# Delta layer: beta sigmoids moved, v times beta moved, chunk sums read from PSUM banks, unread matmuls around the norms

## What is computed

```python
q = _causal_dwconv(x @ Wq, conv_q)      # four taps, then silu; k and v alike
q = q / norm(q);  k = k / norm(k)       # over the 32 of a head
beta = sigmoid(x @ Wb)                  # one per head
Kb, Vb = K * beta, V * beta
A = einsum('bnihd,bnjhd->bnij', Kb, K)
T = inverse-like triangular matrix, row by row from I - tril(A, -1)
W = T @ Kb;  U = T @ Vb
# over the chunks of 64, Sd = diagonal of S:
u_i = u0 - w_i * Sd;  o = q_i * Sd + tril(sum(q_i * k_i)) * u_i
S = S + einsum('bchd,bche->bhde', k_i, u_i)
out = (o * rsqrt(mean(o * o) + EPS) * g) @ Wo
```

## Time and profile before

| what | value |
|---|---|
| time, median of 3 runs | 1680.47 us (1678.34 to 1684.89) |
| the profiled execution | 1683.24 us |
| its span on the core | 1681.5 us |
| mean granted TensorE clock over the span | 0.914 |
| delta layer in it | 1264 to 1464 us |

### The profile page before, as it was taken

How to read it: one execution, slowest core, us unless ns; L and a number is a source line. 1 busy time by engine, 2 the same in 40 slices (tenths; PEclk the granted TensorE clock), 3 DMA queues, 4 the chain that set the end, 5 groups by cost and what they waited for, 6 DMA issues and landing times. The chain is left out here.

```text
span 1681.5 us, 26802 instructions
## 1 busy us (share of the span) xinstructions
PE 1382.7 (82%) x9088; PEld 941.8 (56%) x9088; DVE 1180.0 (70%) x2866; ACT 774.6 (46%) x1412; POOL 731.4 (43%) x921
## 2 busy tenths in 40 slices
PE   4699999956996539997799898899994588389998
PEld 3333333244884327873477676677872377276886
DVE  5877777456556674558799898697778644769776
ACT  2277777730222221216887664545554311064654
POOL 3833332025642017620088787066672141006665
PEclk9699999968997869998899999999997699589999
DMA  1244240000100000100011110564530000164543
GB/s 39 65 116 130 77 139 24 2 26 13 38 26 12 0 26 26 38 13 19 22 45 41 35 45 20 214 134 123 134 105 7 0 1 1 25 216 120 139 131 106
DMA packets 77883, 104.76 MB, mean 62 GB/s; under 512 B 25185, under 2 KB 43121, under 8 KB 77233
## 3 DMA queue, kind: packets, MB, share of 16 engines
q1 hardware_dynamic: 77760, 103.23, 21.7%
HBM read 92.81 MB, written 10.39 MB: 61 GB/s over the span
## 5 line engine op out<-in xcount | busy, mean ns | idle before, releaser
L526 DVE CUSTOM_DVE_ANT_1 la_neg<-bank,la_table 128x512 f32<-128x512 f32 x256 | 166.4, 688 | 41.5 <-PE bank L617 40.8
L1699 POOL TENSOR_TENSOR lh_h_low<-lh_hidden,lh_h_high 128x512 fp32r<-128x512 f32 x84 | 111.3, 1327 | 161.9 <-ACT lh_h_high L1732 161.6
L1412 DVE TENSOR_TENSOR_SCAN le_h<-le_keep,bank 128x512 f32<-128x512 f32 x128 | 152.2, 1209 | 24.0 <-issue 19.6
L1497 PEld LDWEIGHTS bank<-le_diag,le_dtxT 128*128 128x128 f32 x1024 | 125.6, 191 | 57.8 <-issue 41.7
L1699 POOL TENSOR_TENSOR lf_h_low<-lf_hidden,lf_h_high 128x512 fp32r<-128x512 f32 x84 | 111.1, 1325 | 106.6 <-ACT lf_h_high L1732 106.3
L1497 PE MATMUL bank<-le_diag,le_dtxT 128*128 128x128 f32 x1024 | 132.4, 277 | 21.2 <-DVE le_h L1412 13.6
L453 ACT ACTIVATE la_probT<-bank 128x512 f32<-128x512 f32 x256 | 135.6, 605 | 11.4 <-PE bank L636 9.3
L1722 ACT ACTIVATE bank<-bank 128x512 f32<-128x512 f32 x144 | 83.7, 582 | 62.0 <-PE bank L1887 60.3
L1345 ACT ACTIVATE le_keep<-le_dt,le_A 128x512 f32<-128x512 f32 x128 | 87.1, 711 | 17.5 <-DVE le_h L1412 17.5
L1255 POOL TENSOR_TENSOR le_hc<-le_h,le_c_row 128x512 f32<-128x512 f32 x64 | 81.4, 1272 | 30.0 <-issue 20.5
L48 PE MATMUL bank<-ident 128*128 128x512 bf16 x142 | 45.2, 489 | 59.0 <-DVEq L830 40.4
(11 more groups left out here) (570 smaller groups left out, 3611.7 us busy)
## 6 DMA issues: line engine op xcount, KB each, us to landing
lf_weight<-lf_scratch SPq DMA_DIRECT2D x128, 128.0 KB, 3.0
lh_weight<-lh_scratch SPq DMA_DIRECT2D x128, 128.0 KB, 3.2
le_c_row<-le_scratch SPq DMA_DIRECT2D x32, 256.0 KB, 3.1
la_table<-la_scratch SPq DMA_DIRECT2D x4, 1792.0 KB, 7.0
lf_weight<-lf_scratch SPq DMA_DIRECT2D x64, 64.0 KB, 2.2
lh_weight<-lh_scratch SPq DMA_DIRECT2D x64, 64.0 KB, 2.2
la_bias_parts<-la_scratch_parts SPq DMA_DIRECT2D x12, 248.0 KB, 6.2
lb_w1s<-in_L_ffn_w_dram SPq DMA_DIRECT2D x8, 256.0 KB, 2.8
```

Of the source, the lines that this page charges most:

```text
L526: dve.tensor_tensor_reduce(out=neg[:, u % 2, :].rearrange("p (c i) -> p c i", i=P), in0=k.bank[u % RING1][:].rearrange("p (c i) -> p c i", ...
L1412: dve.tensor_tensor_scan(h[:, i, :], keep[:, i, :], k.bank[4 + q % 2][:], 0.0, ALU.mult, ALU.add).then_inc(scanned, 1)
L1497: last = pe.matmul(k.bank[4 + q % 2][:, j * P:(j + 1) * P], dtxT[:, (g * G2 + bb) * TPB + j, c, :], diag[:, d % DIAGS, j, :], start=True, ...
L1699: pool.tensor_tensor(h_low[:, u % RING, :], hidden[:, u % RING, :], h_high[:, u % RING, :].bitcast(F32), ALU.subtract)\
```

## The change

The sigmoids of beta, with their matmuls, go behind the projections of batch 0, and v times beta ahead of the reciprocals. PE gets 14 idle products behind the last convolution, before the norm sums, and 12 more behind the first root, before the spread. W and U go to eight different banks. Of each, only the four first columns of every chunk are copied (`w_first`, `u_first`, 128x32); the product with k reads the bank itself, and batch by batch W and U alternate.

```diff
-        prod = sb("prod", [P, T])
+        prod = sb("prod", [P, 2, T])
+        w_first = sb("w_first", [P, B, NCH, B])
+        u_first = sb("u_first", [P, B, NCH, B])
...
                     act.activation(xp[:, i, b, TAPS - 1:], k.bank[4 + n % 4][:], ACT.Copy).then_inc(in_copied, 1)
-                if b:
+                if b == 0:
+                    for c in range(B):
+                        act.wait_ge(beta_done, c + 1)
+                        act.activation(beta[:, c, :], k.bank[c][:], ACT.Sigmoid).then_inc(beta_ready, 1)
+                else:
                     silu_and_squares(b - 1)
             silu_and_squares(B - 1)
-            for b in range(B):
-                act.wait_ge(beta_done, b + 1)
-                act.activation(beta[:, b, :], k.bank[b][:], ACT.Sigmoid).then_inc(beta_ready, 1)
...
             for b in range(B):
-                act.wait_ge(wu_done, b + 1)
-                act.activation(wT[:, b, :], k.bank[b % 2][:], ACT.Copy).then_inc(w_copied, 1)
-            for b in range(B):
...
+            for b in range(B):
+                dve.wait_ge(act_ready, 3 * (b + 1))
+                dve.wait_ge(beta_ready, b + 1)
+                dve.tensor_tensor(s3[:, 2, b, :], s3[:, 2, b, :], beta[:, b, :], ALU.mult).then_inc(vb_ready, 1)
             dve.wait_ge(act_ready, 3 * B)
...
-            for b in range(B):
-                dve.tensor_tensor(s3[:, 2, b, :], s3[:, 2, b, :], beta[:, b, :], ALU.mult).then_inc(vb_ready, 1)
...
-                dve.tensor_copy(uT[:, b, :], k.bank[2 + b % 2][:]).then_inc(u_copied, 1)
-            dve.wait_ge(u_copied, B)
-            dve.wait_ge(w_copied, B)
-
-            for src, dst in ((wT, ka), (uT, kbv)):
-                for b in range(B):
-                    link(dve.tensor_tensor(prod[:], s3[:, 1, b, :], src[:, b, :], ALU.mult))
-                    link(dve.tensor_reduce(dst[:, b, :], prod[:].rearrange("p (n c) -> p n c", c=CH), AX_X, ALU.add))
+                for i, (bank, dst, start) in enumerate(((k.bank[b], ka, w_first), (k.bank[4 + b], kbv, u_first))):
+                    dve.tensor_copy(start[:, b, :, :], bank[:].rearrange("p (n c) -> p n c", c=CH)[:, :, 0:B])
+                    link(dve.tensor_tensor(prod[:, i, :], s3[:, 1, b, :], bank[:], ALU.mult))
+                    last = dve.tensor_reduce(dst[:, b, :], prod[:, i, :].rearrange("p (n c) -> p n c", c=CH), AX_X, ALU.add)
+                link(last)
...
+                if b == 0:
+                    pe.wait_ge(wbr_ready, 1)
+                    pe.wait_ge(norm.xnT_ready, B)
+                    for c in range(B):
+                        pe.matmul(k.bank[c][:], wbr[:].rearrange("p h d -> p (h d)"), k.xnT[:, c * T:(c + 1) * T], start=True, stop=True)\
+                          .then_inc(beta_done, 1)
...
+            pe.wait_ge(conv_ready, 3 * B)
+            k.idle_products(pe, 14, 3)
             pe.wait_ge(sq_ready, 2 * B)
             lengths(k.bank[0], sq, norm_done)
             lengths(k.bank[1], sq_k, norm_done)
+            pe.wait_ge(root_ready, 1)
+            k.idle_products(pe, 12, 3)
...
-                if b >= 2:
-                    pe.wait_ge(w_copied, b - 1)
-                    pe.wait_ge(u_copied, b - 1)
-                for src, bank in ((kbn, k.bank[b % 2]), (vbn, k.bank[2 + b % 2])):
+                for src, bank in ((kbn, k.bank[b]), (vbn, k.bank[4 + b])):
```

More of the change, by code:

```diff
@@ L2026, in layer_delta @@
         sq_k = wT
-        uT = beta
         o = cT
@@ L2039, in layer_delta @@
                                                                           sem("yT_done"), sem("m_ready"), sem("mT_ready"))
-        t_ready, wu_done, w_copied, u_copied = sem("t_ready"), sem("wu_done"), sem("w_copied"), sem("u_copied")
+        t_ready, wu_done = sem("t_ready"), sem("wu_done")
         qk_ready, qk_done, o_ready, osq_ready, on_done, oroot_ready, on_ready, out_done = (
@@ L2221, in _ @@
                 sdb = bcast(sd[:, b, 0:1], (1, NCH), (0, B))
-                last = dve.tensor_tensor(u0[:, b, :, :], first(wT[:])[:, b], sdb, ALU.mult)
+                last = dve.tensor_tensor(u0[:, b, :, :], w_first[:, b, :, :], sdb, ALU.mult)
             link(last)
-            link(dve.tensor_tensor(u0[:], first(uT[:]), u0[:], ALU.subtract))
+            link(dve.tensor_tensor(u0[:], u_first[:], u0[:], ALU.subtract))
             link(dve.tensor_tensor(u0[:], u0[:], early[:], ALU.mult))
@@ L2253, in _ @@
                     pe.matmul(k.bank[4 + n % 4][:], w3[:, i, :], k.xnT[:, b * T:(b + 1) * T], start=True, stop=True).then_inc(in_done, 1)
-            pe.wait_ge(wbr_ready, 1)
-            for b in range(B):
-                pe.matmul(k.bank[b][:], wbr[:].rearrange("p h d -> p (h d)"), k.xnT[:, b * T:(b + 1) * T], start=True, stop=True).then_inc(beta_done, 1)
+                if b == 0:
[4 more added lines that the diff above has]
+                          .then_inc(beta_done, 1)
             pe.wait_ge(pool_order, 2 + 3 + 1 + B)
```

## The result

The changed kernel took 1676.95 us at the median of 20 runs (1671.82 to 1686.72), the kernel before 1684.91 us at the median of 20 (1673.87 to 1688.06). The ratio on record, which is not the quotient of these two medians, is 0.9962, with a 95% interval of 0.9949 to 0.9976: 0.38% faster, 6.4 us, and no change is outside the interval. The two medians themselves lie 7.96 us apart, and that too is inside the interval (4.0 to 8.6 us). A second set of seven runs, beside the last experiments, gave 0.9933 (0.9907 to 0.9959); its expectation was

The account below looks back on a forecast made before the run. No engine bounds the whole span (PE busiest, 82%); in the layer ScalarE, then VectorE bounds stage by stage. Gains 1.1 + 0.2 + 0.3 + 6.4 = 8.0 us from 1680.47 gave 1672.5 us, bounds 1671.0 to 1675.1, with clock rivals 1668 to 1677.

Parts of the forecast that it names:

- Part 1: Sigmoids moved among the conv's copies: 3.36 us with their table load leave the path, insertion costs 0.
- Part 2: Fourteen idle products before the norm sums: 5.2 us use up the freed 3.4; first root 1.1 us earlier (0.5 to 1.9).
- Part 3: Twelve idle products behind the first root: cost 0, gain 0.2 us at the spreads and 0.3 at the transposes.
- Part 4: v times beta ahead of the reciprocals: 2.49 us move from VectorE's busy time into its wait; gain 0, cost 0.
- Part 5: Chunk sums read from PSUM banks batch by batch: 3.0 us per batch, 6.4 us gained (bounds 3.9 to 7.5).
- Neither level: Clock rivals: PE low through norm sums or W and U, 1674.5 us, chance 0.24; high to the transposes, 1670.4, chance 0.21.
- The bank reads: Rival at the chunk sums: PE's bank writes slow VectorE's bank reads; 1.0 us more per product loses all 8.0; chance 0.05.
- the move of the sigmoids: Rival at the conv: sigmoids delay batch 1's copies past 1285.1, needing 6.2 us where 4 are due; no chance of its own.
- The untouched stage: Sign at 1342 to 1420: over 2 us longer or shorter there would make the whole prediction wrong.
- The sum: Whole kernel: 1.1 + 0.2 + 0.3 + 6.4 = 8.0 us gained, median 1672.5 us, 0.48%.
- the rivals on the clock: PE's clock low (1674.5 us, chance 0.24) or high up to the transposes (1670.4 us, chance 0.21).

Follow-up runs that it names:

- e2: Kernel before with only the beta products and sigmoids moved behind batch 0's projections; ratio 0.9981 (0.9958 to 1.0004).
- e3: Changed kernel without all 26 idle products, run against the kernel before; ratio 0.9935 (0.9910 to 0.9959).
- e1: Kernel before with only the chunk sums changed: W and U in eight banks, read from the banks batch by batch; ratio 0.9951 (0.9931 to 0.9971).
- e10: Kernel before, full copies and four banks kept, but products and sums of W and U done batch by batch; ratio 0.9977 (0.9960 to 0.9994).
- e8: Changed kernel without its 26 idle products, with others in PE's waits at norms, transposes, W and the tail; ratio 0.9900 (0.9863 to 0.9938).
- e11: As e8, with 16 instead of 9 idle products behind the sums of the output's norm; ratio 0.9897 (0.9872 to 0.9922), median 1665.9 us.

## Why the prediction was right or wrong

**Part 1, right.** 3.36 us freed were forecast, 3.50 measured (e2), with no cost at the conv. The sigmoids' table load shows no gap behind it in its new place either: it ended at 1279.95 in e2, and the first sigmoid started at 1279.97. The 1.4 us that the Trainium skill ("ScalarE: Activation LUTs", What ACT_TABLE_LOAD costs) would have added did not appear.

**Part 2, right in mechanism and size.** The batch uses up what part 1 freed: 4.97 us between conv and sums where 5.2 was taken, and the root 1.1 us earlier as forecast; a second profile has 1.55, within the bounds of 0.5 and 1.9. The sums began 0.15 us earlier than forecast and the root followed them by 1.13 us instead of 1.0. It followed that the change would be better without the batch. e3 shows this in the root at 3.83.

**Part 3, cost right, gain not: the one mis-sized term of the gain.** The 12 cost nothing. The 0.2 and 0.3 us credited for spreads and transposes were not there. From the root to k times beta it is 12.55 us in all three profiles. From there to A the changed kernel has 8.44 and 8.32 us; with the order of before it is 8.63, 7.97 (e1) and 8.00 (e10). The term of 0.5 us should have been 0, with the moment at which the clock rose deciding between 7.96 and 8.79. The prediction itself said why: behind the twelve, PE has some 9 us with only the spreads to do. In the changed kernel the clock was back at 0.50 at 1324.6 and stayed there until 1334.9, while the transposes began at 1329.99:

```profile
1325.00:1334.00 9.00, 7.48 (x26) 4.88 (x26) 6.26 (x11) 1.93 (x4) 0.00 (x0) 0.50 0.01 2
```

**Part 4, right:** 0 (e2 against e3).

**Part 5, right:** 6.4 forecast, 6.55 measured (6.4 in the second profile), 3.0 us a batch forecast and 2.95 found ((1434.09 - 1422.28) / 4). The 62 cycles more that the Trainium skill ("VectorE: DVE Perf Modes", The TRN2 errata) gives for a PSUM read did not show: 0.677 us out of the bank, 0.691 in the earlier trace rows out of SBUF.

**The rivals.** Neither level held throughout: the norm sums ran at the high one, the transposes began at the low one, and W and U were at the low one for their first batch alone. The bank reads did not hold VectorE up, and the move of the sigmoids was hidden. The untouched stage, from xx to the first W product, is 0.1 to 0.3 us shorter, so it sets nothing.

**The sum.** With the measured terms it is 1.1 + 0 + 6.55 = 7.65 us, by the second profile 1.55 + 0 + 6.4 = 7.95; the layer's profiles gave 7.3 and 8.4, the ratio of 20 runs 6.4 (4.0 to 8.6). The 8.0 is in that interval, near its upper end. The 20 runs cannot say whether 0.5 or 1.5 us of it are missing, and I leave that open.

**The step that failed is the base of the sum.** The prediction took 8.0 us from 1680.47 us, a median of three runs, and allowed for it to stand 2 us off. With 20 runs the kernel before has 1684.91 us, 4.4 us more. So the forecast of 1672.5 was 4.4 us too low, and the measured 1676.95 lies outside its bounds of 1671.0 to 1675.1, and only just inside the 1668 to 1677 that take in the rivals on the clock, while 1684.91 less 8.0 is 1676.9. That this meets the measured median so closely is luck, since 0.5 us of the 8.0 was not there and two medians of 20 runs are not known to 0.1 us.

**The scale was misjudged as well.** I took 0.5% as about what can be told from no change, and expected with 0.55 to be within it. The ratio of 20 runs has an interval of 0.14% each way, so that even a gain of 0.38% is told from none. Whether it is under 0.5% is less sure: the interval ends at 0.51%, and the second set has 0.67%.

**Where the spread comes from.** The start of the delta layer, up to which all these kernels run the same code, lies anywhere from 1259.15 (changed, second profile) to 1271.43 us (e8) behind the start of the span:

```profile
1259.15 0.35 SPq L2054 DMA_DIRECT2D lg_w<-in_L_attn_b_Wq_dram  x1
```

```profile
1271.43 0.35 SPq L2054 DMA_DIRECT2D lg_w<-in_L_attn_b_Wq_dram  x1
```

That is 12 us of difference in untouched layers, more than the whole change brings. In this stretch PE is busy for 1060.0 us in the first and for 1070.2 in the second with the same 7483 instructions, VectorE for 891.3 and 890.2: most of the difference is in PE's matmuls, at a mean granted clock of 0.93 and 0.92. e8 shows it best: its profiled execution has a span of 1676.0 us, longer than that of the changed kernel, although its own layer is 8.2 us shorter.

## What to carry to other kernels

Unread matmuls that raise PE's clock belong where PE waits anyway. Queued ahead of work that is ready sooner, they delay it until the last has run; here 0.9 us won in the sums could not pay for 3 us of queue. Even in a wait they bring nothing if the clock has fallen again when the work comes. Where one engine waits for the last of many tiles, let it start on the first and read the PSUM bank directly: here the order gave the larger part, the missing copies 2.65 us. When layers ahead of the change vary by more than the change brings, compare the distances between the same instructions within the layer, and take the ratio from many runs.

## What was not expected of the hardware

A VectorE product of 128x512 f32 with one operand in a PSUM bank took 675 to 678 ns, one with both in SBUF 691 ns: the bank was the shorter one, also while PE wrote other banks. And PE's clock fell from 1.00 to 0.50, 0.7 us into the output matmuls, although PE had been busy for 3.63 us with idle products, then 1.14 us with four-row spreads, with only 1.5 us of wait in between (e11).
